# Attention: row maxima turned onto rows in halves of a unit, scores 24 tiles behind the maxima instead of 40

## The reference

```python
KPH = LAT // H            # 8
Q = (hs @ q_w + q_b).reshape(B, S, H, HD).transpose(0, 2, 1, 3)
K = (hs @ k_w + k_b).reshape(B, S, H, KPH).transpose(0, 2, 1, 3)
V = (hs @ v_w + v_b).reshape(B, S, H, KPH).transpose(0, 2, 1, 3)
scores = jnp.einsum('bhsk,bhtk->bhst', Q[..., :KPH], K) / math.sqrt(KPH)
attn = jax.nn.softmax(scores, axis=-1)
ao = jnp.einsum('bhst,bhtv->bhsv', attn, V)
```

## Time and profile before

| | |
|---|---|
| time, median of 3 runs | 3926.04 us (3923.12 to 3926.2) |
| the profiled execution | 3954.11 us, of which the span of the profile is 3952.5 us |
| PE / PEld / DVE / ACT / POOL busy over the span | 84% / 52% / 80% / 61% / 35% |
| L2375 DVE maxima | 1024 x 1222 ns |
| L2353 ACT exponentials | 2048 x 596 ns |
| L2251 and L2273, PE maxima and scores | 2048 each, 453 and 446 ns, side by side |

### The profile page before, as it was taken

How to read it: one execution, slowest core, us unless ns; L and a number is a source line. 1 busy time by engine, 2 the same in 40 slices (tenths; PEclk the granted TensorE clock), 3 DMA queues, 4 the chain that set the end, 5 groups by cost and what they waited for, 6 DMA issues and landing times. The chain is left out here.

```text
span 3952.5 us, 71732 instructions
## 1 busy us (share of the span) xinstructions
PE 3330.8 (84%) x23806; PEld 2070.5 (52%) x23807; DVE 3174.8 (80%) x4210; ACT 2420.0 (61%) x4324; POOL 1370.9 (35%) x957
## 2 busy tenths in 40 slices
PE   8969989897559799987999999999999974299940
PEld 6745555554448689876333333333333332199940
DVE  7859999997866566557999999999999923378868
ACT  6668888785955433310488888888888840133323
POOL 7859999995014444301000000000000006544430
PEclk9979999998879899988799999999999976599975
DMA  7864444444859723296132323232322133223258
GB/s 257 283 198 160 160 161 164 168 161 152 275 180 254 198 75 111 69 280 175 25 72 57 76 54 78 55 78 55 71 61 63 23 96 109 87 84 91 91 177 291
DMA packets 531460, 521.44 MB, mean 132 GB/s; under 512 B 84785, under 2 KB 441265, under 8 KB 531041
## 3 DMA queue, kind: packets, MB, share of 16 engines
q1 hardware_dynamic: 517248, 480.45, 41.6%
q0 software_dynamic: 13952, 37.74, 2.8%
HBM read 301.15 MB, written 215.71 MB: 131 GB/s over the span
## 5 line engine op out<-in xcount | busy, mean ns | idle before, releaser
L2375 DVE TENSOR_REDUCE at_top<-at_psM 128x1 f32<-128x1024 f32 x1024 | 1229.4, 1222 | 22.1 <-PE at_psM L2251 19.1
L2353 ACT ACTIVATE at_probs<-at_psS 128x512 f32<-128x512 f32 x2048 | 1108.9, 596 | 177.4 <-PE at_psS L2273 54.8
L2251 PE MATMUL at_psM<-at_k,at_q 62*128 62x512 f32 x2048 | 756.1, 453 | 29.6 <-DMA at_vraw<-scratch_vf 20.1
L2273 PE MATMUL at_psS<-at_q,at_k 64*128 64x512 f32 x2048 | 756.5, 446 | 0.9 <-ACT at_probs L2353 0.9
L655 POOL TENSOR_TENSOR sc_prod<-sc_state,sc_c_row 128x1024 f32<-128x1024 f32 x256 | 649.1, 2564 | 84.3 <-DVE sc_state L806 72.5
L2289 PE MATMUL at_psV<-at_probs,at_v 128*32 128x256 f32 x8192 | 641.2, 390 | 0.0
L806 DVE TENSOR_TENSOR_SCAN sc_state<-sc_dec,sc_psI 128x1024 f32<-128x1024 f32 x256 | 574.2, 2276 | 43.6 <-PE sc_psI L727 34.7
L2251 PEld LDWEIGHTS at_psM<-at_k,at_q 62*128 62x128 f32 x2048 | 316.9, 190 | 445.7 <-DVE at_top L2375 347.3
L738 PE MATMUL sc_psY<-sc_prod,sc_ident 128*128 128x512 f32 x1024 | 478.4, 597 | 15.2 <-DVE sc_y L792 15.2
L2221 POOL COPY at_v<-at_vraw 128x256 f32<-128x256 f32 x32 | 12.9, 402 | 1182.8 <-DMA at_vraw<-scratch_vf 1182.7
L674 ACT ACTIVATE sc_scaled<-sc_uT,sc_b_col 128x256 f32<-128x256 f32 x768 | 325.2, 494 | 96.2 <-PE sc_psI L727 96.2
(11 more groups left out here) (408 smaller groups left out, 4907.6 us busy)
## 6 DMA issues: line engine op xcount, KB each, us to landing
sc_c_row<-scratch_bc SPq DMA_DIRECT2D x128, 512.0 KB
scratch_xs<-at_zeros SPq DMA_DIRECT2D x140, 264.0 KB, 5.0
sc_b_row<-scratch_bc SPq DMA_DIRECT2D x32, 512.0 KB, 5.0
ec_y<-scratch_ys SPq DMA_DIRECT2D x32, 512.0 KB, 6.1
ex_x<-scratch_xs SPq DMA_DIRECT2D x39, 264.0 KB, 2.8
si_x<-in_x SPq DMA_DIRECT2D x16, 512.0 KB, 5.5
scratch_xn<-si_xn SPq DMA_DIRECT2D x16, 512.0 KB, 6.4
scratch_x_t<-si_xT SPq DMA_DIRECT2D x16, 512.0 KB, 3.1
```

The lines of the kernel that those rows point to most:

```text
L2251: ins = pe.matmul(psM[t % 2][:, half * TILE:(half + 1) * TILE], rows_of(q4[j], h, 0, MAXROW)[:, c * P:(c + 1) * P], rows_of(k4[j], h, 0, M ...
L2273: pe.matmul(psS[e % 3][:], rows_of(k4[j], h, 0, GROUP)[:, c * P:(c + 1) * P], rows_of(q4[j], h, 0, GROUP)[:, half * TILE:(half + 1) * TILE ...
L2353: act.activation(probs[:, slot(u, n), :], psS[e % 3][:], ACT.Exp).then_inc(act_done, 1)
L2375: dve.tensor_reduce(at, psM[t % 2][:], AX.X, ALU.max, negate=True).then_inc(maxed, 1)
```

## The change

A unit is turned in two halves of 16 tiles (512 queries each). `w` counts halves. `minus_max`, `turn`, `turned` and `maxima_rows` run once per half; `maxima_rows` fills one half of the columns of rows 62 and 63, with a DMA for each head and each of the two rows: eight DMAs for a half. The distance of the scores becomes 24 tiles (`HALF + LEAD`): the prologue is 24 tiles. PE waits for `top_in` at steps 0 and 16, and turns at steps 10 and 26. In SP's stream the rows of an odd half (the second of a unit) stand ahead of `store(u, 0)`, those of an even half ahead of `store(u, 1)`. At the start DVE clears the four `k4` and POOL the four `q4`.

```diff
-    TURN = 52
+    HALF = MT // 2
+    TURN = HALF - 6
...
-                if n == TURN and u + 1 < UNITS:
-                    turn_at[u + 1], entries = entries, entries + 1
-    COLLECTED = (18 + LEAD, FIRST + LEAD)
+                if n % 2 == 0 and s % HALF == TURN and (u, s) < (UNITS - 1, HALF):
+                    turn_at[2 * u + s // HALF + 1], entries = entries, entries + 1
+    COLLECTED = (2 + LEAD, 18 + LEAD)
...
-                def maxima_rows(u):
+                def maxima_rows(w):
 
-                    j = u % NQ
-                    sp.wait_ge(act_done, turn_at[u] + 1)
+                    j, half = w // 2 % NQ, w % 2
+                    sp.wait_ge(act_done, turn_at[w] + 1)
                     m.settle(sp)
                     for h in range(QUAD):
-                        dst = rows_of(q4[j], h, MAXROW, 2).bitcast(F32).rearrange("k (c s) -> k c s", s=P)
-                        sp.dma_start(dst, topT[2 * KC * h:2 * KC * (h + 1), :]).then_inc(top_in[j], 16)
+                        for k in range(2):
+                            dst = rows_of(q4[j], h, MAXROW + k, 1)[:, half * TILE:(half + 1) * TILE].bitcast(F32)
+                            src = topT[2 * KC * h + KC * k + KC // 2 * half:2 * KC * h + KC * k + KC // 2 * (half + 1), :]
+                            sp.dma_start(dst.rearrange("k (c s) -> k c s", s=P), src).then_inc(top_in[j], 16)
...
                 for u in range(UNITS):
+                    maxima_rows(2 * u + 1)
                     store(u, 0)
                     if u + 1 < UNITS:
-                        maxima_rows(u + 1)
+                        maxima_rows(2 * u + 2)
                     store(u, 1)
...
-                for j in range(2, NQ):
-                    pool.memset(k4[j][:].bitcast(F32), 0.0).then_inc(zeroed[j], 1)
+                for j in range(NQ):
                     pool.memset(q4[j][:].bitcast(F32), 0.0).then_inc(zeroed[j], 1)
...
-                    v, t = u + 1 + (s + LEAD) // MT, (s + LEAD) % MT
+                    v, t = u + (s + HALF + LEAD) // MT, (s + HALF + LEAD) % MT
...
-                for u, count in ((0, MT), (1, LEAD)):
-                    pe.wait_ge(loaded[u], 16 * LOADS)
-                    for t in range(count):
-                        for half in range(NHALF):
-                            maxima(u, t, half)
+                pe.wait_ge(loaded[0], 16 * LOADS)
+                for t in range(HALF + LEAD):
+                    for half in range(NHALF):
+                        maxima(0, t, half)
                 turn(0)
-                pe.wait_ge(top_in[0], 16 * QUAD)
+                pe.wait_ge(top_in[0], 16 * 2 * QUAD)
...
-                        if u and s == 0:
-                            pe.wait_ge(top_in[u % NQ], (u // NQ + 1) * 16 * QUAD)
+                        if s % HALF == 0:
+                            pe.wait_ge(top_in[u % NQ], (2 * (u // NQ) + s // HALF + 1) * 16 * 2 * QUAD)
...
-                for j in range(2):
+                for j in range(NQ):
                     dve.memset(k4[j][:].bitcast(F32), 0.0).then_inc(zeroed[j], 1)
-                    dve.memset(q4[j][:].bitcast(F32), 0.0).then_inc(zeroed[j], 1)
...
-                def minus_max(u):
+                def minus_max(w):
...
+                    head, rest = split2[:, 0, :, cols], split2[:, 1, :, cols]
...
-                    minus_max(u)
+                        if t % HALF == HALF - 1:
+                            minus_max(2 * u + t // HALF)
```

More of the change, by code:

```diff
@@ L2259, in free, with turn @@
                         pe.wait_ge(act_done, e - 2)
-                def turn(u):
-                    e = turn_at[u]
+                def turn(w):
+                    e = turn_at[w]
                     free(e)
-                    top_at.wait(pe, u, "rest")
+                    top_at.wait(pe, w, "rest")
                     pe.transpose(psS[e % 3][:, 0:P], top2[:], ident[:]).then_inc(keyed, 1)
@@ L2315, in step @@
                         scores(u, n)
-                        if n == TURN and u + 1 < UNITS:
-                            turn(u + 1)
-                for u, count in ((0, MT), (1, LEAD)):
-                    pe.wait_ge(loaded[u], 16 * LOADS)
-                    for t in range(count):
-                        for half in range(NHALF):
-                            maxima(u, t, half)
+                        if half == 0 and s % HALF == TURN and (u, s) < (UNITS - 1, HALF):
+                            turn(2 * u + s // HALF + 1)
+                pe.wait_ge(loaded[0], 16 * LOADS)
+                for t in range(HALF + LEAD):
+                    for half in range(NHALF):
+                        maxima(0, t, half)
                 turn(0)
-                pe.wait_ge(top_in[0], 16 * QUAD)
+                pe.wait_ge(top_in[0], 16 * 2 * QUAD)
                 pe.wait_ge(ones_in, 2 * 16 * NQ)
@@ L2341, in _, with turned @@
                     act.sem_inc(sums_st[half], 16)
-                def turned(u):
-                    e = turn_at[u]
+                def turned(w):
+                    e = turn_at[w]
                     act.wait_ge(keyed, e + 1)
@@ L2359, in _ @@
                             exponential(u, n)
-                            if n == TURN and u + 1 < UNITS:
-                                turned(u + 1)
+                            if n % 2 == 0 and s % HALF == TURN and (u, s) < (UNITS - 1, HALF):
+                                turned(2 * u + s // HALF + 1)
             @block.vector
             def _(dve):
-                for j in range(2):
+                for j in range(NQ):
                     dve.memset(k4[j][:].bitcast(F32), 0.0).then_inc(zeroed[j], 1)
-                    dve.memset(q4[j][:].bitcast(F32), 0.0).then_inc(zeroed[j], 1)
                 dve.memset(ones[:], 1.0).then_inc(ones_made, 1)
@@ L2375, in maximum @@
                     dve.tensor_reduce(at, psM[t % 2][:], AX.X, ALU.max, negate=True).then_inc(maxed, 1)
-                def minus_max(u):
[L2379 to L2384, removed]
+                def minus_max(w):
+                    u, cols = w // 2, slice(w % 2 * (KC // 2), (w % 2 + 1) * (KC // 2))
+                    dve.wait_ge(maxed, w * HALF + HALF)
+                    if w:
+                        dve.wait_ge(act_done, turn_at[w - 1] + 1)
+                    head, rest = split2[:, 0, :, cols], split2[:, 1, :, cols]
+                    top_at.done(dve.tensor_copy(head.bitcast(F32R), top[u % 2][:, :, cols]), "head")
+                    top_at.wait(dve, w, "head")
+                    top_at.done(dve.tensor_tensor(rest, top[u % 2][:, :, cols], head, ALU.subtract), "rest")
                 def collect(u, half):
@@ L2394, in _ @@
                         for half in range(NHALF):
-                            if t == COLLECTED[half] and u >= half + 1:
-                                collect(u - half - 1, half)
+                            if t == COLLECTED[half] and u:
+                                collect(u - 1, half)
                         maximum(u, t)
-                    minus_max(u)
-                collect(UNITS - 2, 1)
+                        if t % HALF == HALF - 1:
+                            minus_max(2 * u + t // HALF)
                 collect(UNITS - 1, 0)
```

## The result

The changed kernel takes 4035.0 us (median; 4031.0 to 4035.9), the kernel before 3925.1 us beside it: ratio 1.0273, 95% interval 1.026 to 1.0286. It is slower, by 109.9 us, where I had forecast +56.5 us and a range that ended at 4012 us.

What follows compares the result with a forecast made beforehand. PE was taken to set the pace at 1.23 us a step, DVE close behind. Terms -20.3 - 2.1 + 2.4 + 14.9 + 61.6 = +56.5 us on 3926.0 gave 3982.5 us, range 3924 to 4012 us.

Steps and rivals of the forecast that it cites:

- the prologue: Ahead of the first turn: sixteen maxima tiles fewer at 1.27 us each, -20.3 us, gained once.
- the start: Phase start: with POOL clearing `q4`, SP's first load no longer waits for DVE's second memset, -2.1 us.
- the first half's rows: Phase start: the first half's eight issues have nothing to hide behind, +2.4 us.
- the price of a turn: In the loop: 32 more turns, each 0.46 us of PE, +14.9 us.
- the even halves: Rows of even halves: 6.4 us needed of the 6.53 us available, just in time, no cost.
- the new wait: Step 16, units 1 to 28: SP reaches the odd half's rows late, PE waits 2.2 us each, +61.6 us.
- the sum's silent one: Behind the waits at step 16: the sum counted only their own length, nothing for a lower clock.
- the clock falls in each wait: Rival, behind each of 28 waits: 1.3 us more, +37 us, 4019 us; chance 0.12 together with the slow queue.
- Cheap issues: Rival, odd halves: eight issues at the loads' price, 2.95 us, wait 0.2 us; sum -1.6 us, 3924 us; chance 0.12.
- the zeros would be a floor: Odd halves, step 16: the last zeros land at 20.3 us into the unit, where the rows are needed.
- 0.4 us for a copy on four engines: Row copies on SP: if the engine split sets the price, eight take 3.5 us, sum about +14 us.
- SP slower behind the zeros: Rival, odd halves: eight issues take 6.6 us, wait 3.8 us, about 4027 us; chance 0.12 together with the clock's fall.

Runs made afterwards that it cites:

- e2: The changed kernel with four copies for a half instead of eight, both rows of a half side by side in `topT`: 3963.1 us, ratio 1.009.
- e6: e2 with the five stores of zeros ahead of the 17 loads in SP's program instead of behind them: 3932.9 us, ratio 1.0017.
- e7: The changed kernel, still with eight copies, with the five stores of zeros ahead of the 17 loads in SP's program: 4043.1 us, ratio 1.0295.

## Why the prediction was wrong

**What held.** What bounds the kernel, the prologue, the start, the first half's rows and the price of a turn came out within 0.2 us each, and the even halves cost nothing. The place of the new wait was right, with its 28 units, its cause (eight issues behind 17 loads and five stores) and its absence at step 0, in unit 0 and in the last three units. The direction followed from that.

**The step that failed** is the sum's silent one: that a wait costs its own length and no more. The prediction had the other case as a rival, *the clock falls in each wait*, priced at +37 us, and gave it, together with a slow queue, a share of 0.12. It measured +43.4 us: 19 units lost 1.4 to 1.5 us, as the phase's start suggested (1.3), and six lost 2.6. Without these 43.4 us the kernel would have come out at about 3992 us, inside the range. Two arguments had kept it small. That 2.2 us was half the wait at the phase's start was a reason about size without a row between: in the changed kernel the one wait of 1.58 us kept the full clock, three of the five from 1.71 to 2.01 us lost it, and so did all 22 from 2.12 us on. That no row showed a fall was no evidence at all: in the main stretch of before PE was never idle, so that trace could not have shown one. The right use of rows 6 would have been as the nearest row, with its price inside the range; the range ended 7 us below that rival. The sign that the prediction had named for this, a step behind the wait longer than 1.23 us, came: step 16 of unit 12 lasts 2.16 us. The Trainium skill, "TensorE: Matmul & The Clock Gate", section "HAM oscillation — how this bites in real kernels", which I had cited against the change, describes a kernel that lost its clock in the DMA wait of every iteration. The trace agrees in 25 of 28 waits, with 0.50 granted behind them; behind the other three the clock stayed at 1.00.

**The term that was mis-sized** is the wait: 2.51 us instead of 2.2, +8.8 us in all. SP came free at 16.4 us on average; I had two units to go by, 16.1 and 16.8 us, and took the lower one. The eight took 5.2 us behind the zeros (4.9 elsewhere; I took 5.0), and landed 1.09 us after the last issue (I took 1.34 from the phase's start). Since the waits stand where the clock was kept in some units and lost in others, this term and the clock's hang together.

**The other rivals.** *Cheap issues* was wrong in its price for eight copies: 0.57 us each and 0.62 from start to start. But its remark that the zeros would be a floor for cheap issues is what e2 ran into: with four cheap issues the rows landed behind the zeros in 26 of 28 units, and e6 shows that the zeros under way were the cause. The Trainium skill, "DMA: Bandwidth & Descriptors", section "Queues, rings and completion order", has the rule that each DMA engine takes the pieces of one queue in the order of issue. The runs agree in part: behind the zeros the rows' first piece moved 2.81 us after the first issue began, and 1.38 us where the zeros had landed; but of the later landing (2.35 us after the last issue for 1.16) most lies behind the last piece. I had cited that rule in the prediction and left it out of what I expected of e2. By the rule of the Trainium skill, same page, on the number of DMA engines (section "Why a DMA increments its semaphore by 16 and not by 1") I had estimated 0.4 us for a copy on four engines; the estimate was mine, and the runs give 0.57 us for that form and 0.61 for the form of two rows. *SP slower behind the zeros* came only in small: single issues took up to 0.85 us, the eight 5.2 instead of 4.9, far from 6.6. The DMA engines did have their hands full there (in the kernel before their busy share is 0.99 from 2420 to 2426, while the zeros of unit 12 go out), but behind the zeros the eight took only 0.3 us longer than elsewhere.

**What stays open.** Why six of the 25 units lost 2.6 us to the lower clock and the others 1.4 to 1.5: the length of the wait does not order them (2.78 us lost 2.63, 3.09 us lost 1.50). What the trace shows is that the granted clock stood at 0.50 twice as long behind these six waits as behind the other 19. Open too is why the news of the rows' landing comes late behind the zeros.

## What to carry to other kernels

A wait that is put on the engine that sets the pace is priced with what follows it: if a trace has never shown that engine idle, it cannot show what idleness does to its clock, and the nearest stretch in which it waited belongs inside the range. When a step is moved to another place of a queue's program, read two lists there: what the issuing engine still has to issue ahead of it, and what the DMA queue still has to carry; curing one uncovers the other. A large transfer that nobody waits for should stand behind the small one that an engine waits for: moving five stores turned +110 us into -5.

## What the runs showed of the hardware

- In the stretch at 2.4 GHz, all 54 waits of PE of 2.1 us and more in the changed kernel, e2 and e7 were followed by 1.2 GHz, with a loss of 1.2 to 2.6 us each. None of the waits up to 1.6 us was, in these kernels and in e6. With twelve matmuls whose result nobody uses in the pause, 27 of 28 units kept 2.4 GHz.
- A copy of four pieces of 512 bytes from SBUF into one partition holds SP for 0.57 us, one of twice those bytes into two partitions for 0.61: the number of copies counts more than their size. Right behind the five stores of zeros an issue of the first form took up to 0.85 us, and in unit 12 of e6 a load right behind them took 0.88 us of SP instead of 0.32.
- Four small copies issued right behind five stores of 264 KB landed 2.35 us after their last issue (1.8 to 2.9); where the stores had landed before, 1.16. The copies' last piece had ended 1.03 us after the last issue (0.77 where the stores had landed): most of the delay was in the news of the landing, not in the bytes.
